# A decoder layer on one core: each second side product ahead of the mixing, with a reordered start and end

## The reference

```python
x = x + attention(layernorm(x), Wq, Wk, Wv, Wo)     # 32 query heads, 8 key/value heads of 128, rope, causal
x = x + fake_quant(layernorm(x)) @ fake_quant(ctx)  # ctx: 2 x 1024 x 1024, 8 bits, scale and zero point given
x = x + experts(layernorm(x))                       # 64 experts of rank 8, the best 16 by a router, softmax gate
```

## Time and profile before

| | |
|---|---|
| median of three runs | 1337.3 us |
| the profiled execution: time | 1336.83 us |
| its span, first to last instruction | 1335.0 us |
| PE busy | 1274.7 us, 95% |
| DVE, ACT, POOL busy | 820.6, 770.9, 613.3 us |
| mean granted PE clock | 0.986 of 2.4 GHz |

### The profile page before, as it was taken

The page is one execution under the profiler, slowest core; times in us unless marked ns, Lnnn a source line. Parts: engine busy times, 40 slices in busy tenths (PEclk is TensorE's granted clock), DMA queues, the critical chain, the costliest instruction groups (busy, mean ns, idle before and its releaser), DMA issues. The chain is left out here.

```text
span 1335.0 us, 19924 instructions
## 1 busy us (share of the span) xinstructions
PE 1274.7 (95%) x7016; PEld 1094.2 (82%) x7025; DVE 820.6 (61%) x1807; ACT 770.9 (58%) x1585; POOL 613.3 (46%) x454
## 2 busy tenths in 40 slices
PE   5899999999999999999999999999799999988998
PEld 4778998888888888888888878888688887665787
DVE  7498224655555556555555565647587688787763
ACT  4322137677767777777777778853233455555540
POOL 4777666678767777677776754310000000111100
PEclk9899999999999999999999999999899999989999
DMA  7033144547759659486485778569673486100001
GB/s 267 9 126 119 64 130 143 178 127 212 206 153 236 194 146 257 124 201 166 119 236 135 172 217 272 188 204 277 214 212 100 141 290 199 46 1 17 33 32 48
DMA packets 117123, 207.42 MB, mean 155 GB/s; under 512 B 10129, under 2 KB 51089, under 8 KB 113441
## 3 DMA queue, kind: packets, MB, share of 16 engines
q1 hardware_dynamic: 112992, 176.79, 40.2%
q0 software_dynamic: 4032, 29.36, 11.8%
HBM read 147.40 MB, written 88.08 MB: 176 GB/s over the span
## 5 line engine op out<-in xcount | busy, mean ns | idle before, releaser
L1234 DVE TENSOR_TENSOR pT_lo<-banks,pT_hi 128x512 fp32r<-128x512 f32 (+1 forms) x192 | 103.6, 595 | 176.5 <-ACT pT_hi L976 176.5
L1628 PE MATMUL banks<-ob_hi,oa_hi 128*128 128x512 f32 x384 | 150.9, 393 | 8.1 <-DVE ob_lo L1271 8.1
L1628 PE MATMUL banks<-ob_lo,oa_hi 128*128 128x512 f32 x384 | 150.4, 392 | 0.0
L1628 PE MATMUL banks<-ob_hi,oa_lo 128*128 128x512 f32 x384 | 150.4, 392 | 0.0
L1586 PE MATMUL banks<-xc,nring_hi_a 128*128 128x512 f32 x448 | 140.0, 394 | 1.3 <-DVE q_made L1184 1.3
L1586 PE MATMUL banks<-xc,nring_hi_b 128*128 128x512 f32 x448 | 139.8, 393 | 0.0
L1825 POOL TENSOR_TENSOR resid<-resid,colterm 128x1024 f32<-128x1024 f32 x8 | 19.7, 2468 | 256.7 <-ACT colterm L1882 172.8
L960 ACT CAST oa_hi<-oraw 128x1024 fp32r<-128x1024 f32 x48 | 50.4, 1050 | 149.3 <-PE banks L1628 134.3
L976 ACT CAST pT_hi<-banks 128x512 fp32r<-128x512 f32 (+1 forms) x192 | 86.5, 526 | 73.9 <-PE banks L1556 73.7
L1243 DVE CUSTOM_DVE_ANT_0 prob<-banks,mask 128x512 f32<-128x512 f32 (+3 forms) x256 | 109.8, 484 | 0.3 <-DVE resid L1162 0.3
L734 POOL TENSOR_TENSOR q_lo<-q_raw,q_hi 128x512 fp32r<-128x512 f32 x64 | 86.4, 1351 | 41.0 <-ACT q_hi L913 41.0
(11 more groups left out here) (245 smaller groups left out, 3466.8 us busy)
## 6 DMA issues: line engine op xcount, KB each, us to landing
q_raw<-qk_dram SPq DMA_DIRECT2D x64, 256.0 KB, 3.9
o_S<-o_st SPq DMA_DIRECT2D x64, 256.0 KB, 4.1
w<-in_L_attn_Wo SPq DMA_DIRECT2D x32, 512.0 KB, 5.4
oraw<-o_S SPq DMA_DIRECT2D x32, 512.0 KB, 3.7
nraw<-in_L_attn_Wq SPq DMA_DIRECT2D x28, 512.0 KB, 5.6
o_S<-o_S POOLq DMA_DIRECT2D x12, 1024.0 KB, 9.8
o_S<-o_N POOLq DMA_DIRECT2D x12, 1024.0 KB, 10.3
resid<-in_x SPq DMA_DIRECT2D x16, 512.0 KB, 6.4
```

What stands on the lines that cost most here:

```text
L1234: nc.vector.tensor_tensor(pT[1][:, sl], turned_chunk(turned, mixed, c), as32(pT[0][:, sl]), ALU.subtract).then_inc(pT_lo, 1)
L1628: ins = nc.tensor.matmul(step_bank(m, t), oa[a][:, s % 2, k, t * P:(t + 1) * P], ob[c][:, s % 2, k, :], start=(q == 0 and k == 0 and i == ...
```

## The change

Three groups of edits.

**Attention.** `place(u, 1)` stands before `mix(u - 1)`, so a unit on PE is scores, first job, second job, mixing, turning. The queues of ACT, DVE, POOL and SP in the attention loop are as they were.

**Start.** Panel 0 takes its products in the order P1, P2, P5, P6, P7, P4, P3 (before P1, P2, P6, P7, P4, P5, P3). Fills may run ahead of their reader by six banks, not four; the sums for P5 and P6 move from POOL to DVE (`t1`, `t2`); tile 3 is normalised on DVE; on DVE `c11(0, .)` comes before `c00(1, .)`.

**Product with Wo and experts.** The last accumulating transfers wait for steps 10, 13, 18 and 24 (before 8, 8, 16, 16), and the pieces of `w11` have a semaphore each; in the experts the statistics of the late tiles are made in pairs, two of them ahead of the first gate, and tile 4's quantised copy stands ahead of the exponentials on ACT; POOL adds the column term to tile t only once DVE has added tile t - 1.

```diff
-ORDER = ([(0, "P1"), (0, "P2"), (1, "P1"), (1, "P2")] + [(s, p) for s in (0, 1) for p in PROD[2:]]
+ORDER = ([(0, "P1"), (0, "P2"), (1, "P1"), (1, "P2"), (0, "P5"), (0, "P6"), (0, "P7"), (0, "P4"), (0, "P3")]
+         + [(1, p) for p in PROD[2:]]
...
-        return banks[:, 2 + f % 4 if f < 24 else 4 + f % 2, :].rearrange("p (k c) -> p k c", c=P)
+        return banks[:, 6 + f % 2 if f in (4, 5) else 2 + f % 4 if f < 24 else 2 + f % 2, :
+                     ].rearrange("p (k c) -> p k c", c=P)
...
@@ POOL, start
+        pool.wait_ge(ln_out_v, 3)
         w_low(0)
...
-        for n in range(TPB):
-            turn_sum(n)
+        pool.wait_ge(t_sum, TPB)
         weight_sum(0, "S3")
+        w_low(4)
+        for t in range(TPB):
+            t4(t)
         weight_sum(0, "S2")
-        for n in range(TPB, 2 * TPB):
-            turn_sum(n)
-        w_low(4)
-        for n in range(2 * TPB, 3 * TPB):
-            turn_sum(n)
...
@@ POOL, product with Wo
-        pool.wait_ge(step_done, PAIRS)
+        pool.wait_ge(step_done, PAIRS + 2)
         accumulate_negated(GROUPS - 2, 1)
+        pool.wait_ge(step_done, PAIRS + 5)
         accumulate_negated(GROUPS - 1, 1)
-        pool.wait_ge(step_done, 2 * PAIRS)
+        pool.wait_ge(step_done, 2 * PAIRS + 2)
         accumulate_negated(GROUPS - 2, 2)
+        pool.wait_ge(step_done, 3 * PAIRS)
         accumulate_negated(GROUPS - 1, 2)
...
@@ DVE, start
+        def t1(t):
+            dve.wait_ge(t3_sum, t + 1)
+            nc.vector.tensor_tensor(right(t, 0), right(t, 0), left(t, 0), ALU.subtract).then_inc(t_sum, 1)
+
+        def t2(t):
+            dve.wait_ge(t_sum, t + 1)
+            dve.wait_ge(w_lo, 5)
+            nc.vector.tensor_tensor(left(t, 0), right(t, 1), left(t, 0), ALU.add).then_inc(t_sum, 1)
...
         for t in range(TPB):
             t3(t)
-        for f in range(8, 24):
+        for t in range(TPB):
+            t1(t)
+        for f in range(8, 16):
+            fill_low(f)
+        for t in range(TPB):
+            t2(t)
+        for f in range(16, 28):
             fill_low(f)
...
@@ PE, attention
             place(u - 1, 2)
             place(u, 0)
+            place(u, 1)
             if u > 0:
                 mix(u - 1)
-            place(u, 1)
             turn_probs(u)
...
@@ experts: POOL, then ACT, then DVE
+            if t >= 1:
+                pool.wait_ge(m_added, 2 * t)
...
+            if i == 1:
+                copy_turned(i + 3)
             exponentials(i)
...
         late_stats(TPB)
+        late_stats(TPB + 1)
         gate(0)
         lows("x", (2, 3))
-        late_scale(TPB)
-        late_stats(TPB + 1)
+        late_scale(0)
```

More of the change, by code:

```diff
@@ L297, in attention @@
     s_added = {n: sem(f"added_{n}") for n in ("S1", "S2", "S3", "S4")}
-    w00_in, w10_in, w11_in, w01_in = ([sem(f"w{n}_in{q}") for q in range(2)] for n in ("00", "10", "11", "01"))
+    w00_in, w10_in, w01_in = ([sem(f"w{n}_in{q}") for q in range(2)] for n in ("00", "10", "01"))
     o_in = [sem(f"o_in{n}") for n in range(2)]
@@ L707, in weight_sum, with t4 @@
                                         ALU.subtract).then_inc(w_sum, 1)
[L709 to L720, removed]
+        def t4(t):
+            pool.wait_ge(t_sum, 2 * TPB)
+            pool.wait_ge(fill_turned, TPB + t + 1)
+            nc.gpsimd.tensor_tensor(left(t, 1), left(t, 1), left(t, 0), ALU.subtract).then_inc(t_sum, 1)
         def k_low(h):
@@ L894, in w_high, with keep_p1 @@
             nc.scalar.copy(wring[:, 0, n % 3, :], factor(s, p)).then_inc(w_hi, 1)
-        def keep_p1(s):
-            for fb in range(2):
+        def keep_p1(s, fbs=(0, 1)):
+            for fb in fbs:
                 act.wait_ge(p_done, done(s, "P1", fb))
@@ L1024, in _ @@
         ln_scale(7)
+        w_high(4)
+        keep_p1(1, (0,))
         for f in range(8, 12):
             fill_high(f)
-        keep_p1(1)
-        w_high(4)
-        for f in range(12, 24):
+        keep_p1(1, (1,))
+        for f in range(12, 28):
             fill_high(f)
         w_high(5)
-        for f in range(24, 28):
-            fill_high(f)
         for n in range(6, len(ORDER)):
@@ L1360, in _ @@
         c00(0, 0)
+        c00(0, 1)
         keep_u(0, 2, 0)
-        fill_low(24)
-        fill_low(25)
         keep_u(0, 2, 1)
-        fill_low(26)
-        fill_low(27)
-        c00(0, 1)
         keep_u(0, 3, 0)
         keep_u(0, 3, 1)
+        c11(0, 0)
+        c11(0, 1)
         c00(1, 0)
@@ L1493, in product @@
                     if s == 0:
-                        pe.wait_ge(fill_lo, FILLED[p])
+                        pe.wait_ge(fill_lo, FILLED["P6"] if p == "P5" else FILLED[p])
+                if s == 0 and p == "P6":
+                    pe.wait_ge(fill_lo, len(FILLS) - 1 + fb)
                 if p == "P1" and s == LASTP:
@@ L1635, in _ @@
         product(0, "P2")
+        product(1, "P1", (0,))
         fills(range(8, 12))
-        product(1, "P1")
+        product(1, "P1", (1,))
         fills(range(12, 16))
@@ L1641, in _ @@
         product(1, "P2", (1,))
[L1642 to L1645, removed]
+        fills(range(20, 26))
+        product(0, "P5", (0,))
         fills(range(26, 28))
+        product(0, "P5", (1,))
         for s, p in ORDER[5:-2]:
@@ L1828, in _, with late_root @@
     def _(act):
-        def late_root(t):
-            act.wait_ge(var2, t - TPB + 1)
-            nc.scalar.activation(lnw[:, 1, t:t + 1], lnw[:, 0, t:t + 1], ACT.Sqrt).then_inc(root2, 1)
+        def late_root(n):
+            act.wait_ge(var2, n + 1)
+            ts = slice(TPB + 2 * n, TPB + 2 * n + 2)
+            nc.scalar.activation(lnw[:, 1, ts], lnw[:, 0, ts], ACT.Sqrt).then_inc(root2, 1)
         def scale_tile(t):
@@ L1953, in late_stats, with late_scale @@
             row_stats(nc, resid, stats, moments, t, link)
[L1954 to L1958, removed]
+            if t % 2:
+                row_scale_in(nc, moments, lnw, slice(t - 1, t + 1), var2)
+        def late_scale(n):
+            ts = slice(TPB + 2 * n, TPB + 2 * n + 2)
+            dve.wait_ge(root2, n + 1)
             row_scale_out(nc, lnw, rstd, ts, link)
@@ L2088, in _ @@
                 quantise(i + 3)
[L2089 to L2090 removed]
+            if i == 2:
+                late_scale(1)
             if i + AHEAD < TT:
@@ L2095, in _ @@
                 lows("x", (2 * i + 2, 2 * i + 3))
-            if i + 5 < TT:
-                late_stats(i + 5)
             add_out(i - 1)
+            if i == 1:
+                late_stats(TPB + 2)
+                late_stats(TPB + 3)
         low("z", TT - 1)
```

43 lines of the change are left out of this document (20 added, 23 removed).

## The result

The changed kernel takes 1414.6 us in the median of four runs (1413.4 to 1416.6), the kernel before beside it 1335.7: ratio 1.059, interval 1.056 to 1.062. The forecast of 1383 had the sign and a little over half of the size; the time lies above its range. The profiled execution has a span of 1413.0 us, 78.0 over that of before.

A forecast was written before the change was run, and what follows sets the result against it. Attention goes at PE's pace, so each new PE wait is paid in full. 1336.8 plus 67 (65.6 lateness, 1.5 clock) minus 21 (start 10, product with Wo 7, experts 4) gives 1383 us, range 1352 to 1406.

The forecast's parts named there:

- Lateness, 48.1 and 17.5: Attention: second jobs wait for late DVE readings, 48.1 us; first steps in units 57 to 63 wait, 17.5; together 65.6.
- T + 1.20: Attention: T is a turning's start; casts move from T + 0.63 to T + 1.19, second jobs could start at T + 5.79.
- P3 behind P5: Attention: job P3 as second job, after P5 was the earlier unit's second, 1.86 us late in 7 units, 13.0.
- counted as spared: Attention: units behind one with three jobs lose nothing, as the job being read has a whole job's time.
- the lower end, 1.6 each: Units 57 to 63: with ACT's delay hidden altogether, first steps would still be late by 1.6 us in seven units.
- The clock, 1.5: Attention: half clock after waits costs 1.5 us, for unit 27 alone; waits of 1.5 us had no such sequel.
- the upper end: Attention: a loss of 85 us, with half clock after 14 waits of over 2 us costing 20.
- The prediction's own sign of being wrong: Attention: wrong if second jobs start at T + 5.8 without a wait, or PE's clock falls below full.
- Start, 10: Start: waits of 3.41 and 3.32 go; 10 of 14 us gained, at least 4; DVE keeps the rest.
- Product with Wo, 7: Product with Wo: the wait of 7.16 goes, 7 us gained, between 2 and 9 with the clock after it.
- Experts, 4: Experts: ACT's earlier copy removes a wait; 4 us gained of 6.6, between -2 and 8.
- The rival "the clock": Some 30 gaps of 1 to 3 us each bring half clock for 1.5 us: 45 more, 1428; chance 0.05.

The follow-up runs named there:

- e2: The kernel before with the attention edit alone (second job ahead of the mixing): 1428.7 us, ratio 1.069 to the kernel before.
- e4: The changed kernel with DVE's reading of a second job P4, P5 or P6 ahead of the low parts: 1377.2 us, ratio 1.031 to the kernel before.
- e3: The changed kernel with ACT's copy of the mixed values moved behind the other casts of its place: 1346.1 us, ratio 1.007 to the kernel before.
- e7: The changed kernel with 8 to 20 useless matmuls ahead of the second job in nine units where PE waits: 1402.6 us, 12.0 below the changed kernel.
- e1: The changed kernel with the attention's old order (mixing ahead of second job), other edits kept: 1322.1 us, ratio 0.989 to the kernel before.
- e6: The changed kernel with attention's old order, plus panel 1's sums and readings earlier on DVE in the start: 1318.0 us, ratio 0.985 to the kernel before.

## Why the forecast was half right

- **Sign and place**: right. e2 puts the whole loss on the move.
- **Lateness, 48.1 and 17.5**: right. The jobs' waits grew by 49.3, the first steps' by 15.8. The mechanism holds step by step: casts at T + 1.20 (said 1.19), P3's reading at T + 8.15 (said 8.1), and with keys and values, in unit 27, at 518.62 with the copy at 516.58, so T + 2.24 (said 2.23). Most parts hold too: P3 behind P5 waits 1.79 (said 1.86), P1 behind P4 1.20 (1.27), P5 behind P2 0.46 (0.54), P7 behind P6 0.35 (0.43). Unit 27 waits 4.74 where the estimate was 3.2, and unit 17, behind one with three jobs and so counted as spared, waits 1.49. In nine of these places (7.7 us) the view names POOL's low factor as the last to come; they have the sizes worked out for the readings, and e4, which moves DVE's readings alone, leaves none of them behind P5 and P6 and 1.4 behind P2. So POOL needs no term of its own there. For the first steps the lower end, 1.6 each without ACT's delay, was wrong: e3 shows none of it left, they were late by ACT's queue alone.
- **The clock, 1.5**: the step that failed. "I take 65.6 and 1.5 for unit 27 alone ..., as waits of 1.5 us stood in attention without such a sequel." It measured 17.4, close to the 20 that I had worked out and kept only as the upper end (14 waits at 1.5 are 21, not 20). Of the changed kernel's waits in attention, eight of the twelve over 2 us lie beside a stretch of half clock (in e2 ten of twelve), two of the eight between 1.79 and 1.90, and none of the thirty shorter ones. The reason given came from waits of 1.5 us in the trace of before; the sum itself had units at 2.3 to 3.3 and those with keys and values, which are nearer to the 3.29 of the earlier trace rows that was followed by half clock. e7 shows by its edit that idling is the cause, for waits of 2.0 to 4.7, and e2 and e1 (below) show that one wait does not settle it. The Trainium skill (TensorE: Matmul & The Clock Gate, Why this matters for your kernels) warns of idle gaps between bursts of matmuls, since the clock falls behind them; the three longest waits here (3.3, 3.8 and 4.7 us) agree, in the changed kernel and in e2. The prediction's own sign of being wrong, PE's clock in attention below full, came true (0.97).
- **Beside the waits, 9.4**: no term. I counted a job's lateness from T + 5.79, when it could have started, and compared it with waits, which the rows count from the end of the last matmul, about T + 5.96. Against what the units grew by at full clock (64.9 + 9.4) the 65.6 was 8.7 too little; that it met the 64.9 so closely is in part luck.
- **Start, 10**: failed, 0.4 (on the average of eight and three profiled executions with the new and the old start, 1.1). "DVE ... is next and keeps the rest" was right as a reason and wrong in size: PE was ahead until it met the readings behind the ropes of panel 0, whose place on DVE the change had left as it was. The diff showed that order; I stopped at the two waits that went. e6 gives 5 of it back.
- **Product with Wo, 7**: 10.4, of which waits 7.2 and half clock 2.9 (half of 5.7). Above the range given, since that had the clock inside and no room for both.
- **Experts, 4**: 2.9 in the changed kernel, 6.7 in e1 with the same waits; the difference is the clock again (9.5 us at half clock with PE at work against none).
- **Sum**: clock 15.9 and what lies beside the waits 9.4 too little, start 9.6 and experts 1.1 too generous, product with Wo 3.4 and lateness 0.7 the other way: 31.9, the whole miss. The time lies 8.6 above the range, so no single one of the three large terms was enough to leave it: with the clock alone at its size the sum is 1399, with the start alone 1393.

The rival "the clock" (1428, 0.05) named the mechanism that was missing, with 45 more where 15.9 more came, and was given too small a chance.

## What to carry to other kernels

Moving work earlier on the engine that sets the pace moves also what it waits for and what it releases: read every queue that it meets (here ACT's and DVE's, which were laid out for the old order) at the new time, and move those in the same edit or not at all. Where the engine was 98% busy at full clock in a stage, a new order has at most the other 2% to win there. A new wait of some 2 us or more is to be priced with the clock behind it, and a wait that goes with what lies next on the engine that becomes late.

## What was not expected of the hardware

The same wait can be followed by half clock in one kernel's execution and not in another's. In the experts the changed kernel and e1_rest run the same instructions; after:

```profile
1305.17 1.77 PE L2173 MATMUL banks<-q,q1T 128*128 128x512 bf16 x6 [3.12 <-DVE resid L2048]
```

with the clock behind it

```profile
1306.00:1310.00 4.00, 4.00 (x12) 1.51 (x11) 2.90 (x9) 0.78 (x1) 0.00 (x0) 0.57 0.35 135
```

and in e1_rest

```profile
1212.19 1.04 PE L2173 MATMUL banks<-q,q1T 128*128 128x512 bf16 x4 [3.11 <-DVE resid L2048]
```

with

```profile
1213.00:1217.00 4.00, 4.00 (x25) 2.56 (x23) 2.92 (x8) 0.86 (x2) 0.00 (x0) 1.00 0.35 135
```

12 matmuls against 25 in the same 4 us. Likewise the wait of 2.35 in unit 20 was followed by full clock, and the same one of 2.32 in e2_move by 0.58:

```profile
443.00:448.00 5.00, 4.62 (x24) 4.05 (x24) 0.38 (x3) 1.81 (x4) 2.99 (x3) 1.00 0.96 254
...
443.00:447.00 4.00, 3.86 (x10) 3.10 (x11) 0.14 (x2) 1.81 (x4) 2.73 (x3) 0.58 0.91 220
```

So a wait gives a chance of half clock and not a fixed price; the sum over a stage is steadier (41.0 us in the changed kernel, 41.0 in e2_move) than any one place. What decides in a single case these runs don't show.
